# Holding the last group of first-pass scores until its own attention starts

## The chip, the cores and the metric

The kernel runs on one core of one Trainium2 chip. The metric is the device time of one execution in microseconds (us), taken as the median of several runs. PE is TensorE (matmuls), PEld its weight loads, DVE is VectorE, ACT is ScalarE, POOL is GpSimd, SP is SyncE, which only issues DMAs here.

## What is computed

Four transformer layers run one after the other on a tensor of 4 sequences x 512 tokens x 288 channels, all in float32. Each layer is, cut to what matters:

```
h  = modulate(layernorm(x), shift, scale)
q, k, v = split(h @ Wqkv + b)                  # 16 heads of 18 channels
a  = softmax(q @ k.T * 18**-0.5)               # per head
x  = x + gate * ((a @ v) @ Wproj + b)
h  = modulate(layernorm(x), shift2, scale2)
x  = x + gate2 * (gelu(h @ W1 + b1) @ W2 + b2) # layer 0: four experts, two per token
```

Layers 0, 1 and 3 attend over 512 tokens of a sequence. Layer 2 works on a reshaped form with short rows, and has other code.

## The kernel before, in words

**Units of work.** One layer of one sequence is a unit `i` from 0 to 15 (layer `i // 4`, batch `i % 4`). The kernel goes through the units in a software pipeline: the loop body of unit `i` issues the attention of `i` with the projections of `i + 1` beside it (`pre`), then the feed-forward part of `i - 1` (`ffn_steps`) with the middle of `i` beside it (`mid`: output projection, residual, second norm).

**Order.** A Python planner, `plan`, writes one list of steps. Every engine then walks through that same list and issues its own part of each step, so each engine works in the planner's order. The planner keeps a clock `pe[0]` of estimated PE time (table `PE_NS`) and uses it only to pace the side streams.

**The two passes over the scores.** The softmax needs the maximum of each row before the exponential. A first pass computes the scores once only for these maxima, and a second pass computes them again with the maximum folded in.

- First pass, `s1_steps(i)`: 32 *visits* per unit, for `p` in 0..7 and `q` in 0..3. One visit is two matmuls of 54x512 (profile line L1762), each into a PSUM bank of its own, and two DVE `reduce_max` over those banks (L1520). Eight visits (two values of `p`) make a *group* `g = p // 2` of four heads. After a group comes `rows`: PE transposes the maxima (L1768), DVE writes them and their rounding remainder (L1526, L1529), and SP issues four DMAs that lay them into the rows of QS (L1129). `rows` is put off (`late`) until the second visit of the next group has been issued.
- Second pass, `at_steps(i)`: 17 steps. Step `st` issues four matmuls of 56x512 (L1775) into two pairs of banks, ACT takes their exponentials (L1369), and the four products with V of the step before follow on PE (L1785). Steps 0-3 belong to group 0, steps 12-15 to group 3. At the start of a group `at_steps` forces the stream until that group's `rows` has been issued.

**Who steps the first pass.** The visits are a generator in the list `stream`. Three places advance it by one visit: each second-pass step (after its four matmuls), `weave` beside the feed-forward part (with a gap of `S1_NS`: 5000 ns of planner time in layer 0, 400 ns in the units behind it), and the forcing above. A visit also needs `pe[0]` to be 12,000 ns past the issue of the loads of its Q and K rows (`QK_LAND`):

```
while not hurry[0] and pe[0] < qk_at.get((i, min(g, 2)), 1e9) + QK_LAND:
    yield
```

**Beside the second pass.** From step 2 on, except in steps 5, 9 and 13 (which transpose a finished group, L1794), each step ends with a piece of unit `i + 1`: steps 2-4 transpose its normed rows (ACT into HF, then DVE L1482 to L1490 into A), steps 6, 7, 8, 10 and 11 project a tile of Q and K (seven matmuls, L1732). Of such a tile ACT copies the high part (L1342), DVE subtracts the low part (L1514) and frees the bank, and SP stores both to DRAM (L1095). SP reads the rows back with `qkin` (L1122): twelve DMAs after the tile of step 7, twelve after that of step 10.

**Banks.** During the second pass the pairs (4,5) and (2,3) hold scores and bank 6 the product. Visits, transposes and projections take turns in `RING_A`, three banks:

```
RING_A = (0, 1, 7)
```

**Where the visits lie.** Followed by its own arithmetic, the planner's order gives this. The numbers are the visits of the last group (8 in all) that are issued ahead of their own second pass: unit 0: none; units 1, 2 and 12: one each; units 3, 4 and 5: none; units 6 and 13: four each; units 7, 14 and 15: three each. The remaining ones are issued one to a step from step 0 on, with one step left out where `rows` of group 2 takes it if that is still due. `rows` of the last group comes in step 9 of units 1, 2 and 12, step 10 or 11 of 3, 4 and 5, step 5 of 6 and 13, and step 6 of 7, 14 and 15. The first visit of the next unit comes in step 12, but in step 13 of units 6, 13 and 14. Units 8 to 11 (layer 2) have no such visits.

Of the kernel before, what the change touches and what calls it, by code (L numbers as in the profile page):

```python
# [34 lines left out]
ST_LAND = 14000  # L35
SP_JOBS = 3
BG = 3
TURN_AT = 2
LEAD = 6
W_MID = 4  # L40
# [38 lines left out]
def plan(full, s_av, s_tn, s_fc2, s_qw):  # L79
# [8 lines left out]
    def put(*a):  # L88
        steps.append(a)
        pe[0] += PE_NS.get(a[0], 0)  # L90
# [20 lines left out]
    def bank(k):  # L111
        settle(k)
        fills[k] += 1
        if in_pair[k]:
            other[k, fills[k] - 1] = (k - 1, in_pair[k])
        return (k, fills[k] - 1)

    def pair(k):
        settle(k)
        settle(k + 1)  # L120
        fills[k] += 1
        if fills[k + 1]:
            other[k, fills[k] - 1] = (k + 1, fills[k + 1])
        in_pair[k + 1] = fills[k]
        return (k, fills[k] - 1)
# [3 lines left out]
    def ring():  # L129
        ring_n[0] += 1  # L130
        return bank(ring_of[0][ring_n[0] % len(ring_of[0])])
# [267 lines left out]

    m_n, m2_wait, mrow = [0] * 4, [None], {}  # L400

    hurry, stream = [False], []

    def s1_step():
        while stream and next(stream[0], "end") == "end":
            stream.pop(0)
# [6 lines left out]
    def s1_steps(i):  # L413
        def rows(g, last):
            bk = ring()
            put("rows", i, g, bk, last, m2_wait[0])
            m_n[g] += 4 * 16
            m2_wait[0] = (g, m_n[g])
            mrow[g] = m_n[g]
            s1_at[0] = (i, g)  # L420

        late = None
        for p in range(H // 2):
            g = p // 2
            for q in range(QT):
                while not hurry[0] and pe[0] < qk_at.get((i, min(g, 2)), 1e9) + QK_LAND:
                    yield
                bks = []
                for x in range(2):
                    bk = ring()  # L430
                    put("s1", i, p, q, x, bk, qk_n[min(g, 2)])
                    bks.append(bk)
                for x in range(2):
                    put("s1_max", p, q, x, bks[x])
                yield
                if late is not None and q == DEFER:
                    rows(*late)
                    late = None
                    yield
            if p % 2:  # L440
                late = (g, bk)
        yield
        rows(*late)
        yield
# [4 lines left out]

    def at_steps(i):  # L450
        exps = {}

        def s2(st):
            g, kt = st // 4, st % 4
            exps[st] = []
            for x in range(2):
                bk = pair(4 - 2 * x)
                put("s2", i, st, x, bk, mrow[g], pb_free[st % 3])
                exps[st].append(bk)
            for _ in range(2 if i == 0 else 1):  # L460
                s1_step()
            if kt == 3:
                s2_done[g] = bk
                s2_at[0] = (i, g)

        def av(st):
            g, kt = st // 4, st % 4
            if kt == 0:
                acc[g] = bank(6)
            for hh in range(4):  # L470
                put("av", i, st, hh, exps[st][hh // 2], v_ready[kt], acc[g])
            if kt == 3:
                pb_free[st % 3] = (full[6], acc[g][1] + 1)
                v_done[0] = acc[g]
                put("os", i, g, acc[g], os_free[0])
            else:
                n_av[0] += 1
                pb_free[st % 3] = (s_av, n_av[0])

        def norm_o(g):  # L480
            bk = ring()
            put("no", i, g, acc[g], bk)
            os_free[0] = bk
            return bk

        acc = {}
        for st in range(17):
            if st < 16:
                hurry[0] = True
                while s1_at[0] is None or s1_at[0] < (i, st // 4):  # L490
                    s1_step()
                if i == 0 and st == 0:
                    for _ in range(LEAD):
                        s1_step()
                hurry[0] = False
                s2(st)
            if st >= 1:
                av(st - 1)
            turned = st >= 2 and (st - 2) % 4 == 3
            if turned:  # L500
                norm_o((st - 2) // 4)
            yield turned
        o_ready[0] = ("rows", norm_o(3))
        yield True
# [39 lines left out]
    def at2_steps(i):  # L544
        exps = {}
        for st in range(2):
            bks = [ring() for _ in range(4)]
            put("s2b", i, (0, 1, 2, 3), st, bks, (mrow[0], mrow[1]))
            for qt in range(4):
                put("s2b_exp", qt, st, bks[qt], pb_free[qt // 2])  # L550
                exps[qt, st] = bks[qt]
            yield
        for g in range(4):
            s2_done[g] = bks[3]
        s2_at[0] = (i, 3)
        for u in range(2):
            bks = (ring(), ring())
            put("av2", i, u, bks, {k: v for k, v in exps.items() if k[0] // 2 == u}, vr[0])
            pb_free[u] = (full[bks[1][0]], bks[1][1] + 1)
            v_done[0] = bks[1]  # L560
            for half in range(2):
                put("os", i, u, bks[half], os_free[0])
                yield
                turned = ring()
                put("no2", i, half, u, bks[half], turned, pb_free[2] if half + u == 0 else None)
                os_free[0] = turned
                yield
        for sub in range(2):
            sw[sub] += 16
            put("scr", i, sub, turned)  # L570
        n_otr[0] += 1
        o_ready[0] = ("landed", n_otr[0])
        if i == 11:
            put("vt1", v_done[0])
        put("otr", i, tuple(sw), n_otr[0], n_o[0], n_turn[0])
        pb_free[2] = ("sw", tuple(sw))
        yield
# [3 lines left out]
    def gates(i, g):  # L581
        put("gates", i, g, gr_ready[i // 4, g], gb_free[g])
        gb_ready[g] += 16
# [35 lines left out]
    def step_bg(n):  # L619
        while n > 0 and bg:  # L620
            if next(bg[0], "end") == "end":
                bg.pop(0)
            else:
                n -= 1
# [14 lines left out]
    def ffn_steps(i, experts=None):  # L639
# [26 lines left out]
        def fc2(x, parts, more):  # L666
            u, hb = hid[x]
            for s_ in parts:
# [22 lines left out]
                if more:  # L691
                    step_bg(BG)
                yield
# [100 lines left out]
    bg += [ada0, split(("wg",), "wg"), split(("p", 0), "p")]  # L794
    bg += [prep_f() for _ in range(NCH)]
    stream.append(s1_steps(0))
    for i in range(NI + 1):
        L, b = i // 4, i % 4
        if i < NI:
# [3 lines left out]
            if i + 1 < NI and (i + 1) // 4 != 2:  # L803
                stream.append(s1_steps(i + 1))
# [7 lines left out]
            for n, turned in enumerate(at2_steps(i) if L == 2 else at_steps(i)):  # L812
                if L == 2 or n >= TURN_AT and not turned:
                    next(nxt, None)
                if n == 3 and i > 1:
                    gates(i - 1, 1)
                step_bg(BG if L == 2 else 2)
                if i == 0 and not gb_ready[0] and (0, 0) in gr_ready:
                    gates(0, 0)
                if i == 0 and n == 8:  # L820
                    put("x", 2)
# [45 lines left out]
def build(nc, x_in, cond, layers, gate_w, out):  # L867
    ctx = ExitStack()
    with ctx:
# [102 lines left out]
        s_out = sem("out_landed")  # L972

        steps, other = plan(full, s_av, s_tn, s_fc2, s_qw)

        pbf = [PB[n][:, :, :].rearrange("p a n -> p (a n)") for n in range(3)]
# [975 lines left out]
```

## Time and profile before

| | |
|---|---|
| median of 3 runs | 2216.1 us (2212.15 to 2219.96) |
| the profiled execution | 2227.37 us, its span 2225.6 us |
| mean granted clock of PE | 0.939 of full speed |
| busy: PE, PEld, DVE, ACT, POOL | 91%, 68%, 60%, 51%, 9% of the span |

"Busy" is the time in which an engine had an instruction in work. Matmuls overlap in the pipeline, so a start-to-start distance says more of PE than a duration. In lines of the trace, `[0.98 <-DVE HH L1514]` means that the engine was idle for 0.98 us before the instruction and that the named work of DVE ended the idle time. PEclk is the granted clock: 1.00 is 2.4 GHz, 0.50 is 1.2 GHz.

### The profile page before, as it was taken

What the parts mean: (1) busy time and instruction counts of PE and PEld (TensorE: products, weight loads), DVE (VectorE), ACT (ScalarE), POOL (GpSimd) and SP (SyncE); (2) the same over time, 40 slices, a digit from 0 to 9 for tenths busy, and PEclk for the clock granted to TensorE, in tenths of its full rate; (3) what the DMA queues carried; (4) which work ended last, traced back from release to release, by engine and by line L of the source; (5) the groups of instructions that cost most, each with busy time, mean ns of one, the idle gap of its engine ahead of it and who ended that gap; (6) DMA issues with size and microseconds to landing.
All of it is one profiled execution on the core that took longest, in us unless ns stands there. A gap on an engine that the chain in (4) does not pass through costs nothing.

```text
span 2225.6 us, 38981 instructions
## 1 busy us (share of the span) xinstructions
PE 2023.0 (91%) x15592; PEld 1502.7 (68%) x15592; DVE 1336.7 (60%) x2940; ACT 1143.4 (51%) x1705; POOL 208.2 (9%) x311
## 2 busy tenths in 40 slices
PE   6988999899998999999899899998997898999998
PEld 4346478748974896698475556887886646474658
DVE  4747647656674677576657582462545858584832
ACT  2353734474555465555726555553344463737363
POOL 2000111111110210011020000001100000000001
PEclk9586999899999999999989999998899999999999
DMA  5234241343234232523331412446155141414111
GB/s 162 56 118 85 72 124 56 75 110 94 72 78 138 60 90 52 141 85 81 97 89 18 123 7 65 69 80 129 33 101 115 25 126 23 102 13 113 17 10 25
DMA packets 204731, 173.97 MB, mean 78 GB/s; under 512 B 54822, under 2 KB 164678, under 8 KB 204550
## 3 DMA queue, kind: packets, MB, share of 16 engines
q1 hardware_dynamic: 197974, 158.76, 30.7%
q0 software_dynamic: 6576, 12.71, 2.1%
q8 instruction: 124, 2.03, 0.4%
q14 instruction: 57, 0.47, 0.1%
HBM read 125.57 MB, written 40.11 MB: 74 GB/s over the span
## 4 chain that ended last, share of the span: by engine, by line
PE 63%; DVE 18%; ACT 11%; DMA 3%; issue 2%; SPq 2%; POOL 0%; ACTq 0%; POOLq 0%; DVEq 0%
PE PSA L1881 16%; PE PSA L1896 14%; DVE MX L1520 8%; PE PSA L1671 5%; PE PSA L1785 5%; PE PSA L1762 5%; ACT PB L1369 4%; PE PSA L1732 4%; PE PSA L1775 4%; PE PSA L1744 2%; PE PSA L1805 1%; DVE HH L1650 1%; PE PSA L1694 1%; ACT FH L1399 1%; DVE FL L1420 1%
## 5 line engine op out<-in xcount | busy, mean ns | idle before, releaser
L1520 DVE TENSOR_REDUCE MX<-PSA 128x1 f32<-128x512 f32 x768 | 490.2, 682 | 289.5 <-PE PSA L1762 285.9
L1881 PE MATMUL PSA<-A,FH 128*128 128x256 f32 x2520 | 444.6, 292 | 14.6 <-DVE HH L1650 10.4
L1896 PE MATMUL PSA<-FH,HH 128*128 128x288 f32 x2016 | 447.9, 313 | 3.3 <-DVE HH L1650 3.3
L1406 ACT ACTIVATE HH<-PSA 128x512 fp32r<-128x512 f32 x252 | 150.6, 598 | 565.0 <-PE PSA L1881 555.5
L1369 ACT ACTIVATE PB<-PSA 128x1024 f32<-128x1024 f32 x384 | 371.0, 1025 | 103.8 <-PE PSA L1775 103.0
L1881 PEld LDWEIGHTS PSA<-A,FH 128*128 128x128 f32 x2520 | 364.9, 195 | 37.1 <-issue 18.6
L1896 PEld LDWEIGHTS PSA<-FH,HH 128*128 128x128 f32 x2016 | 329.0, 195 | 45.1 <-issue 38.5
L1896 PE MATMUL PSA<-FL,HH 128*128 128x288 f32 x1008 | 303.4, 301 | 0.0
L1762 PE MATMUL PSA<-KS,QS 54*128 54x512 f32 x768 | 227.2, 513 | 35.1 <-DVE MX L1520 14.7
L1274 POOL TENSOR_TENSOR X<-X,TM 128x288 f32<-128x288 f32 x128 | 101.3, 809 | 1476.3 <-DVE TM L1585 1476.2
L1785 PE MATMUL PSA<-PB,VT 128*32 128x512 f32 x1536 | 221.9, 643 | 0.0
L1650 DVE TENSOR_TENSOR HH<-PSA,HH 128x512 fp32r<-128x512 f32 x252 | 171.9, 682 | 82.6 <-ACT PSA L1407 82.1
L1881 PE MATMUL PSA<-A,FL 128*128 128x256 f32 x1008 | 207.9, 288 | 7.8 <-DVE FL L1420 7.8
L1775 PE MATMUL PSA<-QS,KS 56*128 56x512 f32 x768 | 167.9, 485 | 34.2 <-ACT PB L1369 17.5
L1896 PEld LDWEIGHTS PSA<-FL,HH 128*128 128x128 f32 x1008 | 196.3, 195 | 0.0
L1762 PEld LDWEIGHTS PSA<-KS,QS 54*128 54x128 f32 x768 | 94.5, 200 | 113.1 <-DVE MX L1520 41.4
L1881 PEld LDWEIGHTS PSA<-A,FL 128*128 128x128 f32 x1008 | 158.9, 194 | 12.2 <-DVE FL L1420 10.8
L1775 PEld LDWEIGHTS PSA<-QS,KS 56*128 56x128 f32 x768 | 68.9, 194 | 143.4 <-ACT PB L1369 72.9
L1407 ACT ACTIVATE PSA<-PSA 128x512 f32<-128x512 f32 x252 | 149.3, 593 | 0.0
L1399 ACT CAST FH<-ST 128x672 fp32r<-128x672 f32 x171 | 125.2, 750 | 12.7 <-PE PSA L1896 11.9
L1420 DVE TENSOR_TENSOR FL<-ST,FH 128x544 fp32r<-128x544 f32 x171 | 125.4, 733 | 5.3
L1732 PE MATMUL PSA<-A,WQ 128*126 128x512 f32 (+1 forms) x300 | 93.9, 415 | 22.3 <-DVE HH L1514 10.4
(171 smaller groups left out, 2252.4 us busy)
## 6 DMA issues: line engine op xcount, KB each, us to landing
qkd<-HH SPq DMA_DIRECT2D x48, 504.0 KB
ST<-in_L_cond_w SPq DMA_DIRECT2D x51, 432.0 KB
ST<-in_L_cond_w SPq DMA_DIRECT2D x102, 192.0 KB
QS<-qkd SPq DMA_DIRECT2D x88, 144.0 KB
KS<-qkd SPq DMA_DIRECT2D x88, 144.0 KB
QS<-qkd SPq DMA_DIRECT2D x144, 72.0 KB
KS<-qkd SPq DMA_DIRECT2D x144, 72.0 KB
ST<-in_L_cond_w SPq DMA_DIRECT2D x153, 48.0 KB
```

The source lines that it names most:

```text
L1369: e.activation(pbf[st % 3][:, p * 1024:(p + 1) * 1024], PSA[:, bk * 512:(bk + 2) * 512], ACT.Exp, scale=SCALE).then_inc(free[bk], 1)
L1406: e.activation(r(HH[u][:, 0, :]), PS[bk][:, :], gelu)
L1407: e.activation(PS[bk][:, :], PS[bk][:, :], gelu).then_inc(s_gelu, 1)
L1420: e.tensor_tensor(r(lo), ST[k % 2][:, s0:s0 + nl], hi[:, 0:nl], ALU.subtract).then_inc(s_wlo, 1)
L1520: e.reduce_max(MX[p // 2 % 2][:, col:col + 1], PS[bk][:, :], axis=AX.X).then_inc(free[bk], 1)
L1650: e.tensor_tensor(r(HH[u][:, 1, :]), PS[bk][:, :], HH[u][:, 0, :], ALU.subtract).then_inc(free[bk], 1)
L1732: m = e.matmul(PS[bk][0:M, :], r(w_), r(x_), start=(z == 0), stop=(z == 6))
L1762: e.matmul(PS[bk][:, :], r(QS[64 * x:64 * x + 54, p, q * 128:(q + 1) * 128]), r(KS[64 * x:64 * x + 54, p, :]), start=True, stop=True).then ...
L1775: m = e.matmul(PS[bk + x][:, :], r(KS[64 * x:64 * x + 56, 2 * g + p, kt * 128:(kt + 1) * 128]), r(QS[64 * x:64 * x + 56, 2 * g + p, :]), s ...
L1785: m = e.matmul(PS[bk][32 * hh:32 * hh + 32, :], VT[:, kt, h * V1:h * V1 + 32], PB[st % 3][:, hh, :], start=(kt == 0), stop=(kt == 3))
L1881: m = e.matmul(PS[bk][:, s_ * 256:(s_ + 1) * 256], r(w_), r(x_[:, half * 256:(half + 1) * 256]), start=(z == 0), stop=(z == 6))
L1896: m = e.matmul(PS[bk][:, 0:C], r(HH[u][:, c, tk]), r(w_), start=False, stop=(j == NCH - 1 and z == 2))
```

## The change

In `s1_steps`, before a visit of group 3, the generator first issues a `rows` that is still due and then yields without issuing anything until `at_steps` of the same unit has begun. `at_steps(i)` says so through `at_now`. A unit whose second pass has begun is not held. Nothing else is changed: the same instructions are issued, in another order.

```diff
+HELD = 3
...
-    hurry, stream = [False], []
+    hurry, stream, at_now = [False], [], [-1]
...
         for p in range(H // 2):
             g = p // 2
+            if g >= HELD and at_now[0] != i:
+                if late is not None:
+                    yield
+                    rows(*late)
+                    late = None
+                while at_now[0] != i:
+                    yield
             for q in range(QT):
                 while not hurry[0] and pe[0] < qk_at.get((i, min(g, 2)), 1e9) + QK_LAND:
                     yield
...
     def at_steps(i):
         exps = {}
+        at_now[0] = i
```

## Rows read from the trace of the kernel before

**Rows 1.** The page, busy time of each engine.
```profile
PE 2023.0 (91%) x15592; PEld 1502.7 (68%) x15592; DVE 1336.7 (60%) x2940; ACT 1143.4 (51%) x1705; POOL 208.2 (9%) x311
```

**Rows 2.** Stretches: window, its us, each engine's busy us, PEclk, DMA share, GB/s.
```profile
1275.00:1314.00 39.00, 36.12 (x223) 27.85 (x223) 35.81 (x78) 15.87 (x26) 1.57 (x2) 1.00 0.11 5
2110.00:2146.00 36.00, 33.45 (x217) 10.70 (x217) 10.87 (x22) 31.82 (x36) 1.55 (x2) 1.00 0.18 22
```

**Rows 3.** Timeline of PE ahead of attention 7: start us, us, instruction, idle before.
```profile
1307.93 0.50 PE L1762 MATMUL PSA<-KS,QS 54*128 54x512 f32 x1
1309.09 0.49 PE L1762 MATMUL PSA<-KS,QS 54*128 54x512 f32 x1 [0.67 <-DVE A L1499]
1309.52 0.54 PE L1896 MATMUL PSA<-FH,HH 128*128 128x288 f32 x2
...
1310.52 0.49 PE L1762 MATMUL PSA<-KS,QS 54*128 54x512 f32 x2
1310.94 0.53 PE L1896 MATMUL PSA<-FH,HH 128*128 128x288 f32 x2
```

**Rows 4.** Timeline of PE ahead of attention 6.
```profile
1190.16 0.49 PE L1762 MATMUL PSA<-KS,QS 54*128 54x512 f32 x1
...
1191.88 0.85 PE L1896 MATMUL PSA<-FH,HH 128*128 128x288 f32 x2
...
1193.62 0.79 PE L1762 MATMUL PSA<-KS,QS 54*128 54x512 f32 x2
1194.35 0.85 PE L1896 MATMUL PSA<-FH,HH 128*128 128x288 f32 x2
```

**Rows 5.** Timeline of DVE and ACT at the start of attention 2.
```profile
439.85 1.28 DVE L1520 TENSOR_REDUCE MX<-PSA 128x1 f32<-128x512 f32 x2
...
442.07 0.22 ACT L1390 ACTIVATE GE<-GL 128x16 f32<-128x16 f32 x1 [9.97 <-DVE GL L1627]
```

**Rows 6.** Second-pass matmuls of attentions 4, 6 and 14: ns min/median/max, first and last start.
```profile
L1775 PE MATMUL PSA<-QS,KS x64: 385/492/502, 861.4 to 909.7; 56*128 56x512 f32 x64
...
L1775 PE MATMUL PSA<-QS,KS x64: 385/492/502, 1199.8 to 1242.9; 56*128 56x512 f32 x64
...
L1775 PE MATMUL PSA<-QS,KS x64: 387/492/503, 2000.6 to 2044.0; 56*128 56x512 f32 x64
```

**Rows 7.** Timeline of PE in attention 4, steps 6 to 8, each step with a visit.
```profile
880.44 1.17 PE L1732 MATMUL PSA<-A,WQ 128*126 128x512 f32 x4 [0.98 <-DVE OT L1539]
...
882.23 0.73 PE L1775 MATMUL PSA<-QS,KS 56*128 56x512 f32 x4
...
885.16 1.19 PE L1732 MATMUL PSA<-A,WQ 128*126 128x512 f32 x4 [0.98 <-DVE HH L1514]
...
886.96 0.73 PE L1775 MATMUL PSA<-QS,KS 56*128 56x512 f32 x4
```

**Rows 8.** Timeline of PE in attention 6, steps 6 to 8, no visit.
```profile
1217.36 1.19 PE L1732 MATMUL PSA<-A,WQ 128*126 128x512 f32 x4 [0.31 <-DVE A L1490]
...
1219.18 0.74 PE L1775 MATMUL PSA<-QS,KS 56*128 56x512 f32 x4
...
1222.67 0.73 PE L1775 MATMUL PSA<-QS,KS 56*128 56x512 f32 x4
```

**Rows 9.** Timeline in attention 14: DVE at step 5, PE at step 6.
```profile
2014.70 0.26 DVE L1536 RECIPROCAL RD<-PSA 128x16 f32<-128x16 f32 x1 [1.55 <-PE PSA L1794]
...
2018.48 1.19 PE L1732 MATMUL PSA<-A,WQ 128*126 128x512 f32 x4 [1.36 <-DVE A L1490]
```

**Rows 10.** Waits of L1775 for the maxima's DMA, in attention 12 and in attention 3.
```profile
  DMA QS<-M: 0.5, 1
...
  DMA QS<-M: 7.6, 2
```

**Rows 11.** The clock: around attention 6's start, and in attention 4 at steps 5 to 8.
```profile
1191.00:1198.00 7.00, 6.68 (x24) 5.20 (x24) 4.10 (x8) 2.81 (x4) 0.00 (x0) 0.54 0.00 0
...
874.00:890.00 16.00, 12.93 (x75) 5.59 (x71) 12.15 (x23) 11.09 (x15) 0.00 (x0) 1.00 0.30 40
```

## The prediction

> **What bounds the kernel now.** I read the page first. PE is busy for 91% of the span and DVE for 60% [rows 1], so on the mean PE is the bound. That is an average over two kinds of stage, so I then read stretches. Beside the feed-forward part ahead of attention 7, DVE is busy for 35.81 of 39 us and PE for 36.12: both are full. In attention 15, where no next unit is projected, DVE is busy for 10.87 of 36 us, ACT for 31.82 and PE for 33.45 [rows 2]. The change carries first-pass visits from the first kind of stage to the second. Last I went through the timelines at the places where a visit leaves and where it arrives. To each of the 12 units with a first pass belongs one seam (the last feed-forward work ahead of its attention) and one attention. Units 0, 3, 4 and 5 have no last-group visit ahead of their attention, so they keep their order but for effects of place. What moves is one visit in units 1, 2 and 12, four in 6 and 13, three in 7, 14 and 15: 3 + 8 + 9 = 20 visits, 40 matmuls and 40 reduces. The work is the same; only its neighbours change.
>
> **What leaves the seams.** Where PE alone sets the pace a visit costs 0.42 us, from 1310.52 to 1310.94 [rows 3]. Ahead of 7, 14 and 15 all three visits lie like that: 3 x 0.42 = 1.3 us per unit, 3.8 us for the three. Ahead of 6 the first of the four runs into a bank that DVE has not freed: it takes from 1190.16 to 1191.88, 1.72 us. The second takes 0.73 us (1193.62 to 1194.35), because PE runs at half clock there; I give the third the same 0.7 and the fourth 0.4 [rows 4]. That is 3.5 us, and 7.1 us for 6 and 13. The lower bound is 8 x 0.42 = 3.4 us, if the bank wait passes on to the next step; I take the rows, since with the visit gone nothing asks for that bank before `rows`, one step later. Units 1, 2 and 12 lose one visit each, 3 x 0.42 = 1.3 us. In unit 2 there is more: the two reduces of that visit take 1.28 us in the middle of the router's chain of small DVE operations, and ACT waits for that chain before it may take the first exponential of the attention [rows 5]. Behind the change they come after the chain: 1.3 us. In all -(3.8 + 7.1 + 1.3 + 1.3) = **-13.5 us**, with -9.8 as the least.
>
> `rows` of group 2 also moves, from behind the second visit of the group to the step after the last visit of group 2. It costs one short transpose on PE wherever it stands, and its DMAs are wanted at step 8, so nothing waits for it. I cost it at nothing in the seams that had it already, and -0.3 +0.3 in units 1, 2 and 12, where it leaves step 1 of the attention for the seam or for step 0.
>
> **What comes into the attentions.** A whole-attention check first. Attention 4 has all eight visits and lasts 48.3 us between its first and last score matmul; attention 6 has four and lasts 43.1; attention 14 has five and lasts 43.4 [rows 6]. So a visit costs at most (48.3 - 43.1) / 4 = 1.3 us, and attention 4 also splits feed-forward weights, which 6 doesn't. By steps:
>
> - Steps 4 to 6 feed DVE. The first projection must wait for DVE to turn the next unit's rows. It starts 19.0 us into attention 4, 17.6 us into 6 and 17.9 us into 14 [rows 6 to 9]. In 14 two more visits (steps 5 and 6) put 2 x 1.28 = 2.6 us on DVE, of which DVE's idle 1.55 us ahead of step 5's reciprocal [rows 9] absorbs most, and the 1.0 left is partly what `rows` no longer takes there. Bounds 0 and 1.0, I take 0.5. So too for 7. Units 6 and 13 get three more visits. Between 18.4 (14 with the addition) and 19.0 (attention 4) I take 18.8: +1.2 us, bounds 0.8 and 1.4.
> - Step 7 is the dear one. With a visit it takes from 882.23 to 886.96, 4.73 us; without one from 1219.18 to 1222.67, 3.49 us [rows 7, 8]. The visit takes two banks of the three and the projection the third, so the next projection gets the bank that the last one had, and waits for DVE to subtract, behind the two new reduces: the idle 0.98 us. Cost 1.24 us in 6, 13 and 14. Behind 7 comes layer 2, where ACT alone empties the bank, so only the visit's 0.42 counts. In 15 nothing is projected.
> - `rows` of the last group goes from step 5 or 6 to step 9: out of DVE's busy steps and into a step of full PE, +0.3 in 9, and -0.3 in step 5 of units 6 and 13; in 7 and 14 it lay inside the wait already counted.
>
> Sum: units 6 and 13: 2 x (1.2 + 1.24) = 4.9. Unit 14: 0.5 + 1.24 + 0.3 = 2.0. Unit 7: 0.5 + 0.4 + 0.3 = 1.2. Unit 15: ACT sets the pace and hides most, 0.3 (bounds 0 and 3 x 0.42 = 1.3). Units 1, 2 and 12: a visit for a transpose, 0.1 each. **+8.7 us**. The bounds of the single steps give 6.3 and 11.1. The whole-attention check at its full 1.3 us for the 14 visits of units 6, 7, 13 and 14 would give 18; I hold that for too much, since it counts attention 4's weight splits as visits.
>
> The queue on SP that `rows` is moved past: in 6, 13 and 14 its four DMAs now stand behind the twelve reads of the next unit's Q and K and are wanted at step 12, three steps later. Attention 12 has just this order, and its score matmuls waited 0.5 us for that DMA; attention 3 shows the bad case, 7.6 in two, that is 3.8 us each by PE and by its weight loads, which wait together [rows 10]. Taken: 0.
>
> Skill and trace differ here. In attention 4, where these bank waits come in every projection step, PE's clock stayed at 1.00 [rows 11]. The Trainium skill (TensorE: Matmul & The Clock Gate, section "A second HAM failure mode: psum-queue depth-cycling") says that short idle times between groups of matmuls which cycle through the banks can make the clock swing between its two levels. By the row the new waits cost what they last; by the page they would cost more, and the sum would end above the time before.
>
> **A side effect.** The first visit of the next unit waits for 12,000 ns of planner time after the `qkin` of step 7. At step 12 of units 6, 13 and 14 that clock stands at 11,810. With `rows` (350) now inside this stretch it stands at 12,160, so that visit goes into step 12, where nothing is projected, and the 21 visits between shift by one: the slot just ahead of the last group, with its 1.59 us from 1307.93 to 1309.52 [rows 3], falls empty in units 7, 14 and 15. Bounds: -3 x (1.59 - 0.1) = -4.5, and 0 if DVE's work there waits for something else. I take the nearer middle, **-2 us**.
>
> Net: -13.5 + 8.7 - 2 = -6.8; since each removed wait can partly turn up again at the next user of the bank, and that can only shrink the gain, I write **-6 us**. The profiled execution of 2227.4 us would become 2221.4; the median of the runs lies 11.3 us below the profiled one, and 2216.1 - 6 gives **2210 us**. A measurement of this kernel can tell about 0.3%, 6.6 us, from no change, so the forecast stands just inside.
>
> **Rivals.**
> 1. *The clock recovers too.* PE runs at 0.54 from 1191 to 1198 [rows 11], right behind the bank waits ahead of attention 6, which this change thins. These 7 us did the work of 3.8, so a stretch like this costs 3.2 us. If it goes in 6 and 13, or in the starts of 1, 2 and 12: -6 -2 x 3.2 = -12.4, 2204 us. For it: the waits stand just before the fall. Against it: the visits ahead that wait for banks stay.
> 2. *Nothing is left.* DVE's wait only moves: the seams give the lower bound -9.8, the attentions take 8.7 and the side effect is 0: -1, 2215 us. For it: 36.12 of 39 us of PE are busy in a seam, so only the visit's own time can be won.
> 3. *The maxima come late (the other side).* In 6, 13 and 14 the DMAs of `rows` are behind twelve reads on SP. If these slip by one step, step 12 waits as attention 3 did: 3 x 3.8 = +11.4, in all +5 us, 2221; with the seams at their lower bound +9, 2225. It decides from 2 us of waiting on average in each, where the gain is gone. Against it: attention 12 has the order and waits 0.5.
> 4. *The clock falls in the attentions.* If the new waits at step 7 brought a stretch of half clock in 6, 13 and 14, at 3.2 us each, the sum is -6 + 9.6 = +3.6, 2220 us. The page of the skill named above speaks for it, rows 11 against it.
>
> **Numbers.** The forecast, -2 to -10 us: 0.52. Rival 1: 0.24. Rival 2: 0.11. Rival 3: 0.09. Rival 4: 0.04. Faster by over 0.3% are rival 1 and the part of the forecast below -6.6 us (0.18): 0.42. Slower by over 0.3%: most of rival 3 and some of 4: 0.09. Within: 0.49. For 8 in 10 the range takes in rival 1's 2204 and rival 2 and the gentler part of 3, and the bounds of the unknown costs: 2202 to 2219. The likeliest case alone is 2206 to 2214.
>
> **What the profile after would show.** Right: eight L1762 pairs in steps 0 to 7 of attentions 6, 7 and 13 to 15; their seams shorter by 3.5 and 1.3 us (or more, with the emptied slot), 6 and 13 longer between first and last L1775 by 2.4 us, 14 by 2.0, 7 by 1.2, 15 by at most 0.5; an idle 0.98 us ahead of the second projection tile in 6, 13 and 14; the first visit of 7, 14 and 15 in step 12. Wrong: a growing wait of L1775 for the DMA of M; half clock inside these attentions; a seam that is no shorter though its visits are gone, with DVE's other work on its chain. The prediction falls above all if seams give less than their rows, or if a few half-clock stretches come or go with the shifted idle times.

## The result and the profile after

The changed kernel takes 2200.7 us (median of 12 runs, 2192.3 to 2208.4) against 2215.3 us (12 runs) for the kernel before: ratio 0.9926, 95% interval 0.9901 to 0.9950 (the ratio is estimated from all runs and isn't the quotient of the two medians). The gain of 14.6 us is 2.4 times the forecast 6, and the time lies below the range's 2202. In a second comparison it was 2197.7 against 2217.8, ratio 0.9903 (0.9865 to 0.9941). The direction was right and the size was not.

First the page of the kernel after: busy times, and the row of the granted clock in 40 slices. Lines of code stand 9 further down than before: L1762 is now L1771, L1775 is L1784, L1520 is L1529, L1732 is L1741, L1514 is L1523.

```profile
PE 2004.8 (91%) x15592; PEld 1496.7 (68%) x15592; DVE 1336.7 (61%) x2940; ACT 1142.4 (52%) x1705; POOL 208.3 (9%) x311
...
PEclk9686999899989999999999999998899999999999
```

The work is the same: DVE's 1336.7 us as in [rows 1]. PE is busy for 18.2 us less with the same 15592 instructions. The mean granted clock is 0.946 in this execution and 0.939 in the profiled one of before; worked out from these and the spans, PE spent about 33 us less at half clock, which by the price found below is some 12 us. Part of that has nothing to do with the change (attention 0 alone had 43 us at half clock before and 36 after), so the two spans (2200.5 and 2225.6) aren't subtracted here; places are compared one by one.

Stretches of the kernel after: 39 us ahead of attention 7, attention 15, attention 2, attention 6, attention 14 (columns as in [rows 2]).

```profile
1261.50:1300.50 39.00, 36.54 (x237) 29.31 (x235) 34.63 (x78) 16.94 (x28) 1.57 (x2) 1.00 0.11 5
2084.40:2120.40 36.00, 33.28 (x222) 10.93 (x221) 13.63 (x26) 31.82 (x35) 1.55 (x2) 1.00 0.17 22
430.10:486.00 55.90, 47.06 (x278) 19.27 (x277) 39.79 (x99) 39.73 (x49) 9.18 (x14) 0.94 0.44 98
1186.00:1234.10 48.10, 45.12 (x277) 18.87 (x276) 29.10 (x67) 36.70 (x44) 1.55 (x2) 1.00 0.34 85
1977.80:2024.30 46.50, 44.22 (x277) 18.27 (x276) 25.43 (x46) 36.36 (x43) 1.55 (x2) 1.00 0.39 101
```

Against [rows 2] DVE's load ahead of attention 7 fell from 35.81 to 34.63 us and PE does 14 more instructions in the same 39 us. In attention 15 DVE took the visits (10.87 to 13.63). In attentions 6 and 14 the clock stays at 1.00.

Second-pass matmuls of attentions 6 and 14 after:

```profile
L1784 PE MATMUL PSA<-QS,KS x64: 385/492/501, 1186.0 to 1231.1; 56*128 56x512 f32 x64
...
L1784 PE MATMUL PSA<-QS,KS x64: 385/493/502, 1977.8 to 2021.3; 56*128 56x512 f32 x64
```

Against [rows 6], 6 grew from 43.1 to 45.1 us: forecast +2.4, measured +2.0. 14 went from 43.4 to 43.5 where +2.0 was forecast. Why the two differ is the first thing that the timeline answers. DVE and PE in attention 14, steps 5 to 8:

```profile
1992.75 0.68 DVE L1499 TENSOR_TENSOR A<-HF,A 32x512 fp32r<-32x512 f32 x1
1993.46 0.26 DVE L1545 RECIPROCAL RD<-PSA 128x16 f32<-128x16 f32 x1
1993.76 0.46 DVE L1548 TENSOR_TENSOR OT<-PSA,RD 128x288 f32<-128x288 f32 x1
1994.13 1.28 DVE L1529 TENSOR_REDUCE MX<-PSA 128x1 f32<-128x512 f32 x2
1994.36 1.19 PE L1741 MATMUL PSA<-A,WQ 128*126 128x512 f32 x4
...
1996.17 0.73 PE L1784 MATMUL PSA<-QS,KS 56*128 56x512 f32 x4
...
1999.10 1.19 PE L1741 MATMUL PSA<-A,WQ 128*126 128x512 f32 x4 [0.97 <-DVE HH L1523]
...
2000.91 0.73 PE L1784 MATMUL PSA<-QS,KS 56*128 56x512 f32 x4
```

Before, DVE did the reciprocal first, after 1.55 us of idling, then the two writes of `rows`, and only then wrote the last rows' low part, for which the first projection waited: it started 17.9 us into the attention [rows 9]. The kernel before:

```profile
2016.24 0.28 DVE L1526 TENSOR_SCALAR M<-PSA 16x128 fp32r<-16x128 f32 x1 [0.79 <-PE PSA L1768]
...
2017.75 0.68 DVE L1490 TENSOR_TENSOR A<-HF,A 32x512 fp32r<-32x512 f32 x1
```

Now the low part (L1499) is done at 1993.4, ahead of the reciprocal, and the projection starts at 1994.36, 16.6 us in. DVE works in the planner's order, so it is the planner that turned the two round. It puts the low part off until the bank that it reads comes up again in the ring, or until the next piece of unit `i + 1`:

```
later(bk[0], put, "turnx_lo", c, slot, bk, f, a_free[slot])
```

The visit in step 5 now takes two banks of the three, so the transpose behind it gets the third, and the low part is written first. Before, step 5 had no visit, and `rows` in step 6 went ahead of the low part. The run hold_6_13 (below) tells the two causes apart: its attention 14 has `rows` in step 5 and no visit there, the low part still comes behind the reciprocal, and the projection starts 16.6 us in all the same:

```profile
1995.68 0.28 DVE L1535 TENSOR_SCALAR M<-PSA 16x128 fp32r<-16x128 f32 x1 [1.51 <-PE PSA L1777]
...
1997.19 0.26 DVE L1545 RECIPROCAL RD<-PSA 128x16 f32<-128x16 f32 x1 [0.92 <-PE PSA L1803]
...
1999.59 1.20 PE L1741 MATMUL PSA<-A,WQ 128*126 128x512 f32 x4 [0.34 <-DVE A L1499]
```

So `rows` leaving step 6 is enough for the 1.3 us. The two more visits add nothing to that in the changed kernel: the reduces of step 5 fall into time in which DVE idled, those of step 6 come behind the low part. The forecast had +0.5. Step 7 is then as dear as forecast: 1996.17 to 2000.91 is 4.74 us, with the idle 0.97 us of [rows 7]. In attention 6, step 7, kernel after:

```profile
1205.86 0.73 PE L1784 MATMUL PSA<-QS,KS 56*128 56x512 f32 x4
...
1208.07 0.68 DVE L1523 TENSOR_TENSOR HH<-PSA,HH 126x512 fp32r<-126x512 f32 x1
...
1208.81 1.19 PE L1741 MATMUL PSA<-A,WQ 128*126 128x512 f32 x4 [0.97 <-DVE HH L1523]
...
1210.61 0.73 PE L1784 MATMUL PSA<-QS,KS 56*128 56x512 f32 x4
```

4.75 us, the figure of attention 4 [rows 7], where step 7 without a visit took 3.49 [rows 8].

What L1784 waited for in attentions 6, 13 and 14 of the kernel after, us and times:

```profile
  DMA QS<-M: 0.6, 1
...
  DMA QS<-M: 1.0, 2
...
  DMA QS<-M: 0.5, 1
```

The maxima come in time, as in attention 12 before [rows 10]. That ends rival 3.

### The profile page after: what moved, and what is told of

It is laid out like the page before. It is cut to its first block, busy times and chain, and to the rows that moved or that the text cites. A ratio compares the mean times of both kernels' runs of the same rounds, so it can differ in the third digit from the quotient of the medians.

```text
span 2200.5 us, 38987 instructions
## 1 busy us (share of the span) xinstructions
PE 2004.8 (91%) x15592; PEld 1496.7 (68%) x15592; DVE 1336.7 (61%) x2940; ACT 1142.4 (52%) x1705; POOL 208.3 (9%) x311
## 4 chain that ended last, share of the span: by engine, by line
PE 61%; DVE 20%; ACT 11%; DMA 3%; issue 3%; SPq 2%; POOL 0%; ACTq 0%; POOLq 0%; DVEq 0%
PE PSA L1890 16%; PE PSA L1905 14%; DVE MX L1529 9%; PE PSA L1680 5%; PE PSA L1794 4%; PE PSA L1771 4%; PE PSA L1741 4%; ACT PB L1378 4%; PE PSA L1784 3%; PE PSA L1753 2%; DVE HH L1659 1%; PE PSA L1814 1%; PE PSA L1703 1%; DVE FL L1429 1%; ACT FH L1408 1%
## 5 line engine op out<-in xcount | busy, mean ns | idle before, releaser
L1529 DVE TENSOR_REDUCE MX<-PSA 128x1 f32<-128x512 f32 x768 | 490.2, 682 | 292.9 <-PE PSA L1771 289.8
L1905 PE MATMUL PSA<-FH,HH 128*128 128x288 f32 x2016 | 443.2, 311 | 3.9 <-DVE HH L1659 3.3
L1771 PE MATMUL PSA<-KS,QS 54*128 54x512 f32 x768 | 221.4, 504 | 29.8 <-DVE MX L1529 12.2
L1794 PE MATMUL PSA<-PB,VT 128*32 128x512 f32 x1536 | 219.2, 636 | 0.0
L1784 PE MATMUL PSA<-QS,KS 56*128 56x512 f32 x768 | 165.1, 480 | 34.2 <-ACT PB L1378 17.6
L1784 PEld LDWEIGHTS PSA<-QS,KS 56*128 56x128 f32 x768 | 67.9, 192 | 141.0 <-ACT PB L1378 70.7
L1771 PEld LDWEIGHTS PSA<-KS,QS 54*128 54x128 f32 x768 | 93.3, 199 | 102.9 <-DVE MX L1529 36.0
L1741 PE MATMUL PSA<-A,WQ 128*126 128x512 f32 (+1 forms) x300 | 94.2, 416 | 25.2 <-DVE HH L1523 13.3
```

The costliest lines, as they stand in the source:

```text
L1529: e.reduce_max(MX[p // 2 % 2][:, col:col + 1], PS[bk][:, :], axis=AX.X).then_inc(free[bk], 1)
L1741: m = e.matmul(PS[bk][0:M, :], r(w_), r(x_), start=(z == 0), stop=(z == 6))
L1771: e.matmul(PS[bk][:, :], r(QS[64 * x:64 * x + 54, p, q * 128:(q + 1) * 128]), r(KS[64 * x:64 * x + 54, p, :]), start=True, stop=True).then ...
L1784: m = e.matmul(PS[bk + x][:, :], r(KS[64 * x:64 * x + 56, 2 * g + p, kt * 128:(kt + 1) * 128]), r(QS[64 * x:64 * x + 56, 2 * g + p, :]), s ...
L1794: m = e.matmul(PS[bk][32 * hh:32 * hh + 32, :], VT[:, kt, h * V1:h * V1 + 32], PB[st % 3][:, hh, :], start=(kt == 0), stop=(kt == 3))
L1905: m = e.matmul(PS[bk][:, 0:C], r(HH[u][:, c, tk]), r(w_), start=False, stop=(j == NCH - 1 and z == 2))
```

## The experiments

All are edits of the changed kernel. Besides the ratio to the kernel before I use two measures. **Clock**: each run has its mean granted clock. Over the 177 runs that list it, with a level for each row of the table, 0.001 of clock goes with 1.55 us, and what is left scatters by 2.6 us. (The 12 runs of the kernel before that go with the changed kernel's first 12 have times only and aren't in it, so that row is set against the runs of before from the other comparisons.) Worked out: 0.001 of 2215 us is 4.4 us at the lower of the two levels, so a microsecond at half clock costs 1.55 / 4.4 = 0.35 us. "At equal clock" is a kernel's level against that of before in this fit, with its 95% interval. It leaves out whatever an edit gains or loses by changing how often the clock falls. **Places**: a seam is the time from the end of the last product with V (L1794 in the new numbering) of one attention to the first L1784 of the next; the time at half clock in it is taken off at 0.36 us each. That is a mean price. Single stretches cost from 0.1 to 0.5 us for each (last section), so such a figure from one trace is good to about 1 us.

| kernel | median us | ratio (95%) | mean clock | at equal clock |
|---|---|---|---|---|
| before (66 runs) | 2219.0 | 1 | 0.945 | 0 |
| changed, 12 runs | 2200.7 | 0.9926 (0.9901-0.9950) | 0.949 | -12.2 ±1.7 |
| changed again, 6 | 2197.7 | 0.9903 (0.9865-0.9941) | 0.951 | -13.1 ±2.3 |
| hold_6_13 | 2212.9 | 0.9966 (0.9944-0.9987) | 0.946 | -4.7 ±1.7 |
| hold_7_14_15 | 2206.5 | 0.9932 (0.9909-0.9954) | 0.949 | -6.9 ±2.3 |
| hold_1_2_12 | 2213.2 | 0.9974 (0.9952-0.9996) | 0.948 | -0.8 ±1.7 |
| hold_2 | 2216.1 | 0.9989 (0.9972-1.0006) | 0.947 | -0.4 ±1.6 |
| no_early_visit | 2204.3 | 0.9927 (0.9899-0.9955) | 0.950 | -7.2 ±2.3 |
| no_early_again | 2203.6 | 0.9923 (0.9893-0.9952) | 0.951 | -7.9 ±2.0 |
| hold_from_second | 2216.2 | 0.9985 (0.9958-1.0013) | 0.946 | -2.4 ±1.6 |
| two_late | 2213.8 | 0.9975 (0.9949-1.0002) | 0.949 | -0.1 ±1.7 |
| two_at_1 | 2205.0 | 0.9941 (0.9920-0.9962) | 0.946 | -11.7 ±2.1 |
| hold_from_23 | 2201.5 | 0.9928 (0.9902-0.9953) | 0.951 | -7.3 ±2.3 |

### The hold in one set of units at a time

```diff
-            if g >= HELD and at_now[0] != i:
+            if g >= HELD and i in (6, 13) and at_now[0] != i:
```

and the same with `(7, 14, 15)` and `(1, 2, 12)`.

> The hold acts in units 6 and 13 only; every other unit keeps the old order, but that the first visit of units 7 and 14 comes a step earlier. Theory A (the seams' own waits, read from the two traces at equal clock): seams of 6 and 13 shorter by 2.5 us each, their attentions longer by 2.3 us each, the seams of 7 and 14 hardly changed, since the emptied slot is filled by the next visit: in all 0 to -2 us against the kernel before. Theory B (the gain is mostly half-clock time that vanishes ahead of 6 and 13, 10 and 7 us of it in the traces): -8 us more, in all about -9 us, with the mean granted clock higher by about 0.004.

> The hold acts in units 7, 14 and 15 only. Theory A: seams of 7, 14 and 15 shorter by 1.3 us each for their three visits, that of 15 by 1.6 more for the slot that its earlier first visit empties; attentions of 14 and 15 longer by 0.2 and 0.7 us: about -4.5 us. Theory B: none of the vanished half-clock time lies here, so no more than the same -4.5 us.

> The hold acts in units 1, 2 and 12 only, one visit each. Theory A: the router's chain of unit 2 is freed of two reduces (-1.3 us), the rest cancels: -1 to -2 us. Theory B: the traces had 7 us less half clock in each of attention 1, seam 2, attention 2 and seam 12; if that comes from the change it is worth up to 3.4 us each: -10 us or more.

The three parts add up: -4.7 - 6.9 - 0.8 = -12.4 ±3.7 us at equal clock, the whole change -12.2. Units 7, 14 and 15 give the most, 6.9 ±2.3 where 4.5 was expected. Units 6 and 13 alone give 4.7 ±1.7, between the two theories (0 to 2, and about 9). Of this the seams less the attentions make (73.9 - 70.9) + (65.5 - 62.2) - 2.0 - 2.6 = 1.7. Most of the rest lies in attentions 7 and 14. Steps 3 to 6 of attention 7 are 1.6 us shorter, which 3.4 us at half clock in its steps 1 and 2 hide. In hold_6_13 the first visit of those units is already issued in step 12 of 6 and 13, every visit behind it shifts by one, and one more than before lies ahead of their attention. Second-pass matmuls of its attention 14:

```profile
L1784 PE MATMUL PSA<-QS,KS x64: 387/492/502, 1982.9 to 2025.0; 56*128 56x512 f32 x64
```

42.1 us instead of 43.4 [rows 6], and its seams 7 and 14 (66.4 and 63.5) are no shorter than before (66.2, 62.7). So without a hold of its own the early visit shortens the attention, since its place in the seam is filled by the next visit. Only with the hold does a place in the seam fall empty.

hold_1_2_12 gained almost nothing at equal clock; its ratio of 0.9974 goes with a higher clock (0.948 against 0.945).

### The early visit taken back

```diff
-                while not hurry[0] and pe[0] < qk_at.get((i, min(g, 2)), 1e9) + QK_LAND:
+                while not hurry[0] and pe[0] < qk_at.get((i, min(g, 2)), 1e9) + QK_LAND + (300 if p == 0 and i in (7, 14, 15) else 0):
```

The first visit of 7, 14 and 15 goes back to step 13; the hold stays.

> The changed kernel with one thing taken back: the first visit of units 7, 14 and 15 again comes in step 13 of the attention before, not in step 12. Theory A: the emptied slot in the seams of 7, 14 and 15 is used again, at the 1.59 us that it took before, so 4 to 5 us of the changed kernel's gain of 15 are lost: -10 us against the kernel before. Rival: the slot is worth only the visit's own 0.42 us each, which ACT hides in step 12 anyway; then -14 us.

> The changed kernel once more, beside its variants on the same chip. Measured before: ratio 0.9926. If a lasting part of the gain is more full-clock time, the mean granted clock over its runs is again about 0.003 above the old kernel's. If that was luck, the clocks agree and the ratio is about 0.995.

> The same kernel as the earlier one without the early first visit of units 7, 14 and 15. By the profiles the seams of these units are longer by 1.3 to 2.3 us without it. At equal granted clock it should be 4 to 5 us slower than the changed kernel of this call; if the slot is worth only a visit's own PE time, less than 1 us.

The ratios alone don't separate the two: 0.9923 against 0.9903, with intervals that overlap, and a first comparison gave no difference. At equal clock it is 7.2 and 7.9 against 12.2 and 13.1, so the early visit is worth 4.9 ±1.8 us. The seams say so by place, each the mean of two traces: 64.9, 61.4 and 61.9 us for 7, 14 and 15 without it, 62.6, 59.5 and 59.6 with it, 2.3, 1.9 and 2.3 us, 6.5 in all (5.3 if the time at half clock isn't taken off). The changed kernel's own clock is higher again in its second six runs, 0.951 against 0.945, as was expected if that part of the gain lasts. PE and DVE at the end of seam 7, early visit taken back:

```profile
1296.62 0.49 PE L1771 MATMUL PSA<-KS,QS 54*128 54x512 f32 x1
1297.04 0.68 DVE L1508 TENSOR_TENSOR A<-PSA,A 32x512 fp32r<-32x512 f32 x1
...
1297.78 0.49 PE L1771 MATMUL PSA<-KS,QS 54*128 54x512 f32 x1 [0.67 <-DVE A L1508]
...
1298.20 0.54 PE L1905 MATMUL PSA<-FH,HH 128*128 128x288 f32 x2
```

The same place in the kernel after, the last visit of seam 7 and the first score matmul:

```profile
1295.42 0.50 PE L1771 MATMUL PSA<-KS,QS 54*128 54x512 f32 x2 [0.64 <-DVE A L1505]
...
1300.52 0.50 PE L1784 MATMUL PSA<-QS,KS 56*128 56x512 f32 x2
```

The visit from 1296.62 to 1298.20, 1.58 us, is the one of 1.59 us in [rows 3]: its second matmul waits for the bank that DVE turns rows from. After, it isn't there. What the visits waited for in seam 15, first with the early visit taken back:

```profile
L1771 PE MATMUL PSA<-KS,QS x42: 491/498/783, 2031.2 to 2081.8; 54*128 54x512 f32 x42
...
  DVE MX L1529: 1.9, 3
  DVE A L1508: 1.7, 2
```

and in the changed kernel, run beside it:

```profile
L1771 PE MATMUL PSA<-KS,QS x40: 463/498/793, 2031.1 to 2079.3; 54*128 54x512 f32 x40
...
  DVE MX L1529: 1.0, 2
```

One visit less, its wait for L1508 gone (1.7 us by PE and its weight loads together), and one wait for the maxima (L1529) gone too, 0.9 us by both together. The forecast had the first alone.

### Unit 2 by itself

```diff
-            if g >= HELD and at_now[0] != i:
+            if g >= HELD and i == 2 and at_now[0] != i:
```

> The hold in unit 2 alone: one visit leaves the middle of the router's chain. The theory by now: ACT gets the router's logits 1.3 us sooner, PE's idle time at the start of attention 2 shrinks, and with it the half-clock time inside attention 2, 10 to 14 us in the traces without this hold and 6.8 in all with it. Expected: attention 2 with 6.8 us at half clock, 2 to 4 us faster than the kernel before. Rival: the half-clock time falls where it likes and only the 1.3 us or less are won.

No change that can be told (-0.4 ±1.6 at equal clock). In the kernel after, ACT's wait for the router's chain of DVE is 8.86 us instead of 9.97 [rows 5]:

```profile
434.88 0.21 ACT L1399 ACTIVATE GE<-GL 128x16 f32<-128x16 f32 x1 [8.86 <-DVE GL L1636]
```

The wait is 1.1 us shorter (forecast 1.3), but the seam is only 0.1 to 0.7 us shorter. What did change is the clock inside attention 2. The kernel before:

```profile
436.60:495.00 58.40, 49.07 (x277) 19.32 (x273) 39.62 (x99) 39.91 (x49) 9.12 (x14) 0.88 0.41 92
```

and hold_2:

```profile
426.40:482.50 56.10, 47.10 (x278) 19.25 (x277) 39.78 (x99) 39.73 (x49) 9.23 (x14) 0.94 0.44 99
```

Worked out, 0.12 x 58.4 / 0.5 is 14 us at half clock, and 0.06 x 56.1 / 0.5 is 7. By the clock's own records it is 13.7 and 6.8: in nine traces of kernels that hold unit 2's visits from the first 6.8 us; in four that don't, hold_from_second among them, 10.2 to 13.7. This is one of two places where time at half clock went with the edit (the other is ahead of attention 13, below), and it is worth (10.2 to 13.7, less 6.8) x 0.36 = 1.2 to 2.5 us. The runs of hold_2 can't tell that from nothing.

### Holding from another visit on

hold_from_second lets the first visit of the group go ahead and holds from the second; to keep the early visit, the data gate of 7, 14 and 15 is 300 ns lower:

```diff
-            if g >= HELD and at_now[0] != i:
+                if (p, q) == (2 * HELD, 1) and at_now[0] != i:
...
+                while not hurry[0] and pe[0] < qk_at.get((i, min(g, 2)), 1e9) + QK_LAND - (300 if p == 0 and i in (7, 14, 15) else 0):
```

hold_from_23 holds group 2's last visit as well and takes two visits in steps 0 and 2:

```diff
+                while (p, q) == (5, 3) and i in (6, 7, 13, 14, 15) and at_now[0] != i:
+                    yield
...
-            for _ in range(2 if i == 0 else 1):
+            for _ in range(2 if i == 0 or st in (0, 2) and i in (6, 7, 13, 14, 15) else 1):
```

> The hold begins one visit later, so one visit of the last group stays ahead and step 7 of the attention has none (units 1, 2 and 12 are then as in the old kernel; the early first visit of 7, 14 and 15 is kept by a gate that is 300 ns lower there). If the price of step 7 is what the traces show, 1.24 us in units 6, 13 and 14 against 0.42 us in the seam, it is 2 to 3 us faster than the changed kernel, less 1.3 us that unit 2 loses: -1 us. If the visit that stays meets the bank wait of the seams of 6 and 13 again, +1 to +3 us.

> The changed kernel, with the last visit of group 2 held too in units 6, 7, 13, 14 and 15; step 0 takes two visits, step 2 takes rows of group 2 and a visit, the rest keeps its step. The slot that leaves the seam now took 1.1 us (2.1 ahead of 13) in the trace after, and steps 0 to 2 have idle PE while ACT works through the first exponentials. Expected -3 to -5 us against the changed kernel. Rival: the added work on DVE delays the projection of step 6 by as much, 0; the wait then only moves.

One visit less held lost nearly all: 0.9985, and -2.4 ±1.6 us at equal clock. The visit that stays costs again in the seams (6: 71.8 us instead of 69.7 and 70.5; 14: 61.8 instead of 59.5). Step 7 becomes short again, and a new wait shows. PE in step 12 of its attention 6:

```profile
1219.48 0.73 PE L1784 MATMUL PSA<-QS,KS 56*128 56x512 f32 x4
...
1221.83 0.59 PE L1771 MATMUL PSA<-KS,QS 54*128 54x512 f32 x2 [1.62 <-DMA KS<-qkd]
...
1224.21 1.22 PE L1784 MATMUL PSA<-QS,KS 56*128 56x512 f32 x4
```

The early visit waits 1.62 us for its own K and Q rows. The cause is the order on SP. With one visit less to do, `rows` of the last group comes in step 8 instead of 9, and its four DMAs stand ahead of the twelve reads and not behind them. SP in hold_from_second, then in the changed kernel:

```profile
1208.13 2.66 SPq L1138 DMA_DIRECT2D QS<-M  x4
...
1214.17 2.11 SPq L1131 DMA_DIRECT2D QS<-qkd  x6
```

```profile
1215.31 2.09 SPq L1131 DMA_DIRECT2D QS<-qkd  x6
...
1219.63 2.67 SPq L1138 DMA_DIRECT2D QS<-M  x4
```

Counted from the start of attention 6 the reads begin at 31.0 us here and at 29.3 in the changed kernel, where the early visit doesn't wait. In attention 13 the wait is 2.02 us, and behind both waits the clock is at half for 3.4 us. This kernel thus mixes several effects, so it doesn't price the one visit. One visit more held (hold_from_23) makes attentions 6, 13, 14 and 15 longer by 1.1 to 1.8 us and only seam 13 clearly shorter, by 1.1 to 2.1: -7.3 at equal clock, 5 us worse than the changed kernel, though its clock of 0.951 hides this in the median.

### Where the visits go inside the attention

two_at_1 takes step 7's visit into step 1; two_late takes two visits in each step behind 12:

```diff
-            for _ in range(2 if i == 0 else 1):
+            for _ in range(2 if i == 0 else {1: 2, 7: 0}.get(st, 1) if i in (6, 12, 13, 14) else 1):
```

```diff
+            for _ in range(2 if i == 0 or st > 12 else 1):
```

> The changed kernel, but in units 6, 12, 13 and 14 step 1 takes two visits of the held group and step 7 none; rows stays in step 9, so the early first visit and the DMAs keep their times. If the price of a visit beside a projection is the wait for DVE behind the bank (step 7: 4.7 us with, 3.5 without), each of the four attentions is 0.7 to 1.2 us shorter: -3 to -5 us against the changed kernel. If the second visit of step 1 stalls on its bank as long, 0.

> The changed kernel with two visits instead of one after the score matmuls of steps 13, 14 and 15, so that three more visits of the next unit lie in its predecessor's attention and not in the seam. If a seam is bound by DVE, each saves up to 1.28 us there, in the nine units that follow such an attention 2 to 3 us each at most; the added four banks' worth of visits in a ring of three costs a wait for DVE of about 0.7 us a step. Expected: -5 us against the changed kernel; if PE is what bounds both places, 0 to +5 us.

In two_at_1 step 7 fell from 4.8 to 3.5 us in attention 6, and step 1 grew from 2.6 to 4.4. PE and DVE there:

```profile
1185.41 0.63 PE L1771 MATMUL PSA<-KS,QS 54*128 54x512 f32 x3
...
1186.40 2.45 DVE L1529 TENSOR_REDUCE MX<-PSA 128x1 f32<-128x512 f32 x4
...
1187.12 0.50 PE L1771 MATMUL PSA<-KS,QS 54*128 54x512 f32 x1 [1.08 <-DVE MX L1529]
```

Two visits want four banks of three, so the fourth matmul waits for a reduce: the wait of 0.97 us became one of 1.08. Nothing was gained (-11.7 ±2.1 against -12.2 and -13.1). two_late made most attentions with a next first pass 2 to 4 us longer and the seams up to 3.5 shorter, and with that lost the whole gain (-0.1 ±1.7). Its clock is above that of the kernel before beside it by 0.0046 ±0.0021, which is why the ratio still reads 0.9975. None of these beats the changed kernel.

## Why the prediction missed

**The seams, forecast -13.5, measured about -11.3.** As means over the traces with and without the hold there, seam 6 gave 3.2 and seam 13 2.9 (forecast 3.5 each); the hold alone gave 7, 14 and 15 1.3 to 1.5 each (forecast 1.3). These rows carried the forecast well, and the lower bound of 0.42 us a visit in 6 and 13, and with it rival 2, fell. Unit 1 gave 0.6, unit 2 0.4 where 1.7 stood, and unit 12 can't be read in a seam of 400 us.

**The attentions, forecast +8.7, measured +6.7.** 6 and 13 came at +2.0 and +2.6 for 2.4: step 7 grew by 1.3 in both (forecast 1.24), and the first projection came 0.4 later in 6 and 1.3 later in 13 (forecast 1.2 each). The term that failed is "I take 0.5. So too for 7": attention 14 came at +0.2 for +2.0 and 7 at 0.0 for +1.2. In 14 the first projection starts 1.3 us earlier, not later. The term took DVE's list as it stood and added reduces to it; in fact `rows`, which held up the low part in step 6, leaves that step, and the planner sets the low part ahead of the reciprocal and of step 6's reduces. The planner's list for unit 7 changes in the same way, and its step 6 fell from 5.6 to 4.6 us. The bounds of this term, 0 and 1.0, excluded a gain without a reason. 15 came at +0.7 for 0.3; 1 and 12 at +0.9 and +0.3 for 0.1 each.

**The side effect, forecast -2, measured -6.5 by place, -4.9 ±1.8 at equal clock.** This is the largest miss. The mechanism was read right, place included: the visit in step 12, the empty slot of 1.59 us in 7, 14 and 15. "I take the nearer middle, -2 us" is the step that failed: the row said 1.59, the row was right, and a second wait of 0.5 us or so lay behind it. Rounding -6.8 to -6, because a removed wait "can only shrink the gain", was wrong the same way.

These give -11.3 + 6.7 - 6.5 = -11.1 us. The fit gives -12.2 ±1.7 and -13.1 ±2.3, so the account by place is complete to about 1 to 2 us.

**The clock.** The changed kernel's 18 runs have a mean clock of 0.9492, before 0.9451: 4.1 x 1.55 = 6 us. Rival 1 had this recovery, at 0.24, in 6 and 13 or in the starts of 1, 2 and 12. In 6 it isn't borne out: the seam has 13.7 to 23.9 us at half clock without the hold there and 6.8 to 17.1 with it. In 13 it is, in part. Ahead of attention 13, the kernel before and the one after:

```profile
1881.00:1889.80 8.80, 8.18 (x32) 6.34 (x34) 5.59 (x10) 2.76 (x4) 0.00 (x0) 0.61 0.68 113
```

```profile
1858.80:1867.60 8.80, 6.95 (x47) 5.68 (x47) 6.33 (x13) 7.13 (x11) 0.00 (x0) 1.00 0.39 106
```

Seam and attention 13 together have 6.8 to 10.2 us at half clock in the five traces in which that unit keeps visits ahead, and 0 to 10.2, on average 4.3, in the eight in which it keeps none: 4.6 ±3 us less, worth 1.6. Attention 2 (above) is worth 1 to 2.5 us. Where the rest comes from stays open: hold_7_14_15 has the higher clock too (0.949), two_at_1, which is nearly the changed kernel, doesn't (0.946), nor does hold_6_13 (0.946). With 6 to 12 runs whose clocks scatter by several thousandths I can't tie it to one edit. The price, 3.2 us for 7 at half clock or 0.46 for one, was right for a dense stretch and too high for the mean of all runs, 0.35.

**Rival 3** fell by the waits for M. **Rival 4** fell as a regular cost, not altogether. The changed kernel's first trace has no half clock in attentions 6, 7, 13, 14 and 15. Its second has 3.4 us of it in attention 13, behind a wait of 0.98 us of the first projection and ahead of step 7:

```profile
1884.80:1888.20 3.40, 3.40 (x9) 2.25 (x11) 2.00 (x4) 0.12 (x1) 0.00 (x0) 0.50 0.03 5
```

That attention took 48.1 us instead of 46.5 between its first and last score matmul. The same wait is in the first trace, at full clock. In two_at_1 6.8 us at half clock begin in attention 13 beside step 1's new wait. By the rule weighed in the prediction (the Trainium skill, TensorE: Matmul & The Clock Gate, "A second HAM failure mode: psum-queue depth-cycling") such waits can make the clock swing. The stretch of attention 6 with its 0.97 us wait has 1.00, and so have most of its kind; there the trace disagrees, as in [rows 11]. Whether the few stretches above come from such waits no run shows.

So -11.1 by place and -6 of clock, 17 us in all where the two comparisons of medians gave 14.6 and 20.1, against -6 forecast. Of the 5.1 by place that the forecast lacks, 4.5 is the side effect and 0.8 the rounding; seams and attentions missed by 2.2 and 2.0 with opposite signs, and that these cancel is luck. The chances were 0.42 for faster by over 0.3%, and the range ended at 2202 because rival 1 was added to a net that was already too small.

## What to carry to other kernels

When a row shows what an instruction costs in its slot (1.59 us) and the change empties the slot, take the row, not the middle between it and nothing; caution belongs in the range. When a planner writes the order, print the list again for the changed kernel before adding work to a step: here the move took `rows` out of the way and turned two pieces of DVE's work round, and PE's next wait became shorter although DVE had more to do. And where runs list their granted clock, look at a gain of 0.3% at equal clock as well: hold_1_2_12 and two_late read 0.25% faster, and at equal clock they gain nothing. Whether an edit brings the higher clock is a question of its own; two_late's is clear of the scatter, and its cause isn't shown.

## What the runs showed of the hardware

The mean granted clock of one and the same kernel differs by several thousandths from run to run (0.948 to 0.956 in six runs of the changed kernel), and at 1.55 us for each this is most of the scatter: 2192.6 us at 0.956, 2197.9 and 2200.8 at 0.948. A stretch without half clock repeats itself closely: attention 7, up to its last product with V, took 46.7 us before and 46.6 or 46.7 in the ten other traces that have no half clock in it. What half clock costs depends on the place. Between the two traces of the changed kernel, 3.4 us of it made attention 13 1.6 us longer (48.1 us between its first and last score matmul instead of 46.5) and seam 15 only 0.4 (61.0 instead of 60.7).
